# Attention in three wide pieces of 103 keys across heads, with values brought by DMA and masked, whole-tile passes on VectorE, and the output bias as a product

## What is computed

```python
q, k, v = project(norm(x)), project(ctx), project(ctx)    # heads: (32, 16, 128, 8), (32, 16, 77, 8)
scores = q @ k.T / sqrt(8)                                # (32, 16, 128, 77); masked in layer 3
weights = softmax(scores, -1)
o = (weights @ v).merge_heads()                           # (32, 128, 128)
x = x + gate * (o @ Wo + bo)                              # bo in layers 1 and 3
```

## Time and profile before

| | |
|---|---|
| median of three runs | 1613.0 us (1606.56 to 1613.46) |
| profiled execution, own time | 1609.98 us |
| its span | 1608.2 us |
| busy: TensorE, VectorE, GpSimd, ScalarE | 1233.3, 1004.2, 888.1, 821.8 us |
| mean granted TensorE clock | 0.883 of 2.4 GHz |
| l1x, first transfer or table load to last aggregate | 221.2 to 393.7 us |
| l2x | 754.3 to 926.7 us |
| l3x | 1034.2 to 1228.3 us |

### The profile page before, as it was taken

The page is one execution under the profiler, slowest core; times in us unless marked ns, Lnnn a source line. Parts: engine busy times, 40 slices in busy tenths (PEclk is TensorE's granted clock), DMA queues, the critical chain, the costliest instruction groups (busy, mean ns, idle before and its releaser), DMA issues. The chain is left out here.

```text
span 1608.2 us, 27318 instructions
## 1 busy us (share of the span) xinstructions
PE 1233.3 (77%) x9890; PEld 857.0 (53%) x9890; DVE 1004.2 (62%) x2128; ACT 821.8 (51%) x1584; POOL 888.1 (55%) x1106
## 2 busy tenths in 40 slices
PE   4773569997459996444899968689997774989994
PEld 4432546664359994333566535455656553565553
DVE  5789869995531111344999769688882687443421
ACT  2487448886635453144788766467775431212120
POOL 5200148885245554651677578367775345478775
PEclk9796779999679998667899979889997795999997
DMA  2000000000238883110000000000000004344442
GB/s 102 7 0 0 1 2 2 2 2 5 59 111 240 238 230 85 40 31 9 2 1 2 2 16 1 2 2 1 2 2 1 24 33 146 76 80 97 94 88 23
DMA packets 51798, 74.98 MB, mean 47 GB/s; under 512 B 8169, under 2 KB 31602, under 8 KB 51282
## 3 DMA queue, kind: packets, MB, share of 16 engines
q1 hardware_dynamic: 35858, 55.01, 10.7%
q0 software_dynamic: 15808, 18.24, 6.8%
HBM read 57.09 MB, written 16.12 MB: 46 GB/s over the span
## 5 line engine op out<-in xcount | busy, mean ns | idle before, releaser
L1616 PE MATMUL ps<-topk_up_sb,topk_wu 128*128 128x512 f32 x256 | 124.1, 632 | 2.9 <-DVE sb_xnT L1736 2.2
L1517 ACT ACTIVATE topk_ga<-ps 128x512 f32<-128x512 f32 x64 | 38.3, 599 | 155.5 <-PE ps L1616 152.7
L1440 POOL DMA_INDIRECT out<-topk_shared,l3f_route_slots x64 | 100.2, 1566 | 18.1 <-issue 18.0
L1736 DVE TENSOR_TENSOR sb_xnT<-topk_ga,ps 128x512 f32<-128x512 f32 x64 | 43.9, 688 | 103.3 <-ACT topk_ga L1517 99.7
L207 POOL TENSOR_SCALAR sb_stage<-sb_x,l0f_rstd,l0f_shift 128x128 f32<-128x128 f32 x48 | 24.6, 525 | 146.3 <-DVE l0f_shift L194 146.1
L2095 DVE TENSOR_TENSOR l1f_g_y<-ps,l1f_g_wd 128x256 f32<-128x256 f32 x39 | 16.6, 425 | 136.1 <-PE ps L2038 100.2
L2065 ACT ACTIVATE l1f_g_h<-ps,l1f_g_wd 128x256 f32<-128x256 f32 x156 | 63.3, 475 | 73.6 <-DMA l1f_g_wd<-l1f_W 49.9
L522 POOL TENSOR_TENSOR l3x_prob<-l3x_prob,l3x_rden 128x1232 f32<-128x1232 f32 x32 | 72.0, 2249 | 51.1 <-DVE l3x_rden L674 51.1
L522 POOL TENSOR_TENSOR l2x_prob<-l2x_prob,l2x_rden 128x1232 f32<-128x1232 f32 x32 | 72.0, 2249 | 44.4 <-DVE l2x_rden L674 44.4
L634 ACT ACTIVATE l3x_pt<-ps 77x512 f32<-77x512 f32 x128 | 72.7, 592 | 39.7 <-PE ps L576 39.7
L522 POOL TENSOR_TENSOR l1x_prob<-l1x_prob,l1x_rden 128x1232 f32<-128x1232 f32 x32 | 72.0, 2249 | 32.5 <-DVE l1x_rden L674 32.5
(11 more groups left out here) (500 smaller groups left out, 3588.5 us busy)
## 6 DMA issues: line engine op xcount, KB each, us to landing
l1f_g_wd<-l1f_W SPq DMA_DIRECT2D x39, 322.0 KB
l1f_g_wu<-l1f_W SPq DMA_DIRECT2D x39, 256.0 KB
topk_wu<-l3f_W SPq DMA_DIRECT2D x16, 512.0 KB
l1f_y_rows<-l1f_g_y SPq DMA_DIRECT2D x39, 128.0 KB
topk_wd<-l3f_W SPq DMA_DIRECT2D x16, 256.0 KB
...
```

Of the source, the lines that this page charges most:

```text
L1440: pool.indirect_dma_start(out=out_rows, out_offset=spot(g, i), in_=y[g % 2][:, i, :], in_offset=None, compute_op=ALU.add).then_inc(y_added ...
L1517: sc.activation(gx[c % 2][:], ps[:, 2 * (c % 2), :], ACT.Gelu).then_inc(x_acted, 1)
L1616: ins = pe.matmul(ps[:, 2 * (c % 2) + i, :], wu[g % W][:, (i * CX + c) * P:(i * CX + c + 1) * P], xgT[g % 2][:], start=True, stop=True)
L1736: v.tensor_tensor(xh[g % 2][:, c, :], gx[c % 2][:], ps[:, 2 * (c % 2) + 1, :], ALU.mult).then_inc(x_ready, 1)
```

## The change

- **Pieces.** The 308 weights of a group's four heads are cut into pieces of 103, 103 and 102, across the borders of the heads. A piece is turned in four transposes of 103 (or 102) columns, copied as 103 x 512, and weighed in one product a group. There are three pieces in place of four.
- **Values.** For the product of a piece its rows must hold the values of (head, key) in the piece's order. Seven DMAs for each group of four tiles, from SyncE, copy rows of `vall` within SBUF to `vrows` (103 rows, 3 pieces, 4 tiles x 128 columns; two buffers). GpSimd multiplies them by a mask (`vmask`, made once in a stage by six instructions) into `vpad`, 103 x 384, with all features of heads other than the row's own set to zero. The padded values and their clearing in `constants` go.
- **VectorE.** Maximum, subtraction and sum are one instruction of 1232 elements each, and so is the exponential on ScalarE. The statistics' first step moves between maximum and subtraction, the second between sum and reciprocal.
- **Bias.** The bias row is loaded to one partition; a product of a row of ones with it goes ahead of the output product in PSUM. GpSimd's addition of the bias goes, and its wait for the load; TensorE waits for the load once, ahead of the loop.

The core of the diff:

```diff
+    PIECES, L = 3, 103
+    FROM = [(0, 0, 0, 77), (0, 77, 0, 26), (1, 0, 26, 51), (1, 51, 0, 52), (2, 0, 52, 25), (2, 25, 0, 77), (2, 102, 0, 1)]
+    MV = 4
...
-        pt, oT = sbs("pt", [KEYS, HG, GROUPS, P], 2), sbs("oT", [P, P], 2)
+        pt, oT = sbs("pt", [L, PIECES, GROUPS, P], 2), sbs("oT", [P, P], 2)
...
-        bo, gb = sbs("bo", [P, D], 1)[0], sbs("gb", [P, D], 1)[0]
+        vrows, vpad, gated = sbs("vrows", [L, PIECES, MV * P], 2), sbs("vpad", [L, PIECES, P], 2), sbs("gated", [P, D], 2)
+        own_head, vmask = sbs("own_head", [L, PIECES, HG], 1)[0], sbs("vmask", [L, PIECES, P], 1)[0]
+        bo = sbs("bo", [1, D], 1)[0]
...
+        scores = ps[:, 2:6, 0:GK].rearrange("p b (h k) -> p b h k", k=KEYS)
+
+        def piece(g, c):
+            return slice(GK * g + L * c, GK * g + min(L * c + L, GK))
...
+            for j in range(NT // MV):
+                if j >= 2:
+                    sp.wait_ge(vpad_ready, MV * (j - 1))
+                for c, row, key, n in FROM:
+                    sp.dma_start(vrows[j % 2][row:row + n, c, :], t["vall"][key:key + n, j * MV * P:(j + 1) * MV * P]).then_inc(v_here[j % 2], 16)
...
                     pool.wait_ge(heads_made, n - 1)
-                pool.tensor_copy(bass.AP(tensor=vpad[n % 2], offset=0, ap=[[HEADS * 32, KEYS], [HG * 32, GROUPS], [32 + HD, HG], [1, HD]]),
-                                 t["vall"][:, n * P:(n + 1) * P].rearrange("k (g i c) -> k g i c", g=GROUPS, i=HG)).then_inc(vpad_ready, 1)
+                j = n // MV
+                if n % MV == 0:
+                    pool.wait_ge(v_here[j % 2], 16 * len(FROM) * (j // 2 + 1))
+                pool.tensor_tensor(vpad[n % 2][:], vrows[j % 2][:, :, (n % MV) * P:(n % MV + 1) * P], vmask[:], ALU.mult).then_inc(vpad_ready, 1)
...
-            def bias(n):
-                xb = t["x"][:, n * P:(n + 1) * P]
-                pool.tensor_tensor(xb, xb, gb[:], ALU.add).then_inc(biased, 1)
...
-            if bias_out:
-                pool.wait_ge(loads, 16)
-                pool.tensor_scalar(gb[:], bo[:], t["gate"][:, gate_at:gate_at + 1], None, ALU.mult).then_inc(gb_ready, 1)
-                pool.wait_ge(gb_ready, 1)
+            step = Chain(pool, mask_step)
+            step(pool.memset(own_head[:], 1.0))
+            step(pool.affine_select(out=own_head[:], in_=own_head[:], compare_op=ALU.is_ge, fill=0.0, base=0,
+                                    pattern=[[L, PIECES], [-KEYS, HG]], channel_multiplier=1))
+            step(pool.affine_select(out=own_head[:], in_=own_head[:], compare_op=ALU.is_ge, fill=0.0, base=KEYS - 1,
+                                    pattern=[[-L, PIECES], [KEYS, HG]], channel_multiplier=-1))
+            for c in range(PIECES):
+                step(pool.tensor_copy(vmask[:, c, :].rearrange("k (g i c) -> k g i c", g=GROUPS, i=HG),
+                                      own_head[:, c, :].unsqueeze(1).unsqueeze(3).broadcast_to([L, GROUPS, HG, HD])))
...
-            def turn(n, r):
-                if r == 0:
+            def turn(n, c):
+                if c == 0:
                     pe.wait_ge(normed, n + 1)
-                if 4 * n + r >= 2:
-                    pe.wait_ge(turned_kept, 4 * n + r - 1)
+                k = PIECES * n + c
+                if k >= 2:
+                    pe.wait_ge(turned_kept, k - 1)
+                weights = prob[n % 4][:].rearrange("p h k -> p (h k)")
                 for g in range(GROUPS):
-                    ins = pe.transpose(ps[0:KEYS, 6 + r % 2, g * P:g * P + P], prob[n % 4][:, HG * g + r, :], t["ident"][:])
+                    at = piece(g, c)
+                    ins = pe.transpose(ps[0:at.stop - at.start, 6 + k % 2, g * P:g * P + P], weights[:, at], t["ident"][:])
                 ins.then_inc(turned, 1)
 
-            def weigh(n, r):
-                if r == 0:
+            def weigh(n, c):
+                if c == 0:
                     pe.wait_ge(vpad_ready, n + 1)
                     if n >= 1:
                         pe.wait_ge(heads_kept, n)
-                pe.wait_ge(turned_kept, 4 * n + r + 1)
+                pe.wait_ge(turned_kept, PIECES * n + c + 1)
+                rows = min(L, GK - L * c)
                 for g in range(GROUPS):
-                    ins = pe.matmul(ps[32 * g:32 * g + 32, 0, 0:P], vpad[n % 2][:, HG * g + r, :], pt[n % 2][:, r, g, :],
-                                    start=(r == 0), stop=(r == HG - 1), tile_position=(0, 32 * g))
-                if r == HG - 1:
+                    ins = pe.matmul(ps[32 * g:32 * g + 32, 0, 0:P], vpad[n % 2][0:rows, c, 32 * g:32 * g + 32], pt[n % 2][0:rows, c, g, :],
+                                    start=(c == 0), stop=(c == PIECES - 1), tile_position=(0, 32 * g))
+                if c == PIECES - 1:
                     ins.then_inc(heads_made, 1)
...
                 if n >= 1:
                     pe.wait_ge(out_kept, n)
-                pe.matmul(OUT, oT[n % 2][:], w[:, 384:512], start=True, stop=True).then_inc(out_made, 1)
+                if bias_out:
+                    pe.matmul(OUT, t["ones"][0:1, :], bo[:], start=True, stop=False)
+                pe.matmul(OUT, oT[n % 2][:], w[:, 384:512], start=not bias_out, stop=True).then_inc(out_made, 1)
...
@@ -604,19 +616,16 @@
                 weigh(n, 0)
                 turn(n, 2)
                 weigh(n, 1)
-                turn(n, 3)
-                weigh(n, 2)
                 if n + AHEAD < NT:
                     score(n + AHEAD)
-                weigh(n, 3)
+                weigh(n, 2)
...
             def exponent(n):
-                for i in range(2):
-                    sc.wait_ge(shifted, 2 * n + 1 + i)
-                    sc.activation(prob[n % 4][:, 8 * i:8 * i + 8, :], prob[n % 4][:, 8 * i:8 * i + 8, :], ACT.Exp, scale=scale).then_inc(exped, 1)
+                sc.wait_ge(shifted, n + 1)
+                sc.activation(prob[n % 4][:], prob[n % 4][:], ACT.Exp, scale=scale).then_inc(exped, 1)
...
-                for r in range(HG):
-                    if r == 2 and n >= 1:
+                for c in range(PIECES):
+                    if c == 2 and n >= 1:
                         keep_out(n - 1)
-                    sc.wait_ge(turned, 4 * n + r + 1)
-                    sc.activation(pt[n % 2][:, r, :, :].rearrange("k h q -> k (h q)"), ps[0:KEYS, 6 + r % 2, :], ACT.Copy).then_inc(turned_kept, 1)
+                    k, rows = PIECES * n + c, min(L, GK - L * c)
+                    sc.wait_ge(turned, k + 1)
+                    sc.activation(pt[n % 2][0:rows, c, :, :].rearrange("k g q -> k (g q)"), ps[0:rows, 6 + k % 2, :], ACT.Copy).then_inc(turned_kept, 1)
...
+            def largest(n):
+                v.wait_ge(scored, n + 1)
+                v.tensor_reduce(rowmax[n % 2][:].rearrange("p (b h) -> p b h", h=HG), scores, X, ALU.max).then_inc(maxed, 1)
+
             def shift(n):
-                v.wait_ge(scored, n + 1)
-                for i in range(2):
-                    v.tensor_reduce(heads(rowmax[n % 2], i), scores(i), X, ALU.max).then_inc(maxed, 1)
                 if n >= 4:
-                    v.wait_ge(turned, 4 * (n - 3))
-                for i in range(2):
-                    v.wait_ge(maxed, 2 * n + 1 + i)
-                    v.tensor_tensor(probs(n, i), scores(i), heads(rowmax[n % 2], i).unsqueeze(3).broadcast_to([P, 2, HG, KEYS]),
-                                    ALU.subtract).then_inc(shifted, 1)
+                    v.wait_ge(turned, PIECES * (n - 3))
+                v.wait_ge(maxed, n + 1)
+                v.tensor_tensor(prob[n % 4][:].rearrange("p (b h) k -> p b h k", h=HG), scores,
+                                rowmax[n % 2][:].rearrange("p (b h) -> p b h", h=HG).unsqueeze(3).broadcast_to([P, GROUPS, HG, KEYS]),
+                                ALU.subtract).then_inc(shifted, 1)
 
             def total(n):
+                v.wait_ge(exped, n + 1)
+                v.tensor_reduce(rowsum[n % 2][:], prob[n % 4][:], X, ALU.add).then_inc(summed, 1)
+
+            def invert(n):
                 if n >= 2:
                     v.wait_ge(normed, n - 1)
-                for i in range(2):
-                    v.wait_ge(exped, 2 * n + 1 + i)
-                    v.tensor_reduce(rowsum[n % 2][:, 8 * i:8 * i + 8], prob[n % 4][:, 8 * i:8 * i + 8, :], X, ALU.add).then_inc(summed, 1)
-                v.wait_ge(summed, 2 * n + 2)
+                v.wait_ge(summed, n + 1)
                 v.reciprocal(rden[n % 2][:], rowsum[n % 2][:]).then_inc(recip, 1)
 
...
             for n in range(NT):
-                if n + AHEAD - 1 < NT:
-                    shift(n + AHEAD - 1)
-                if n >= 2:
-                    spread(n - 2)
-                if n + AHEAD - 2 < NT:
-                    total(n + AHEAD - 2)
-                if n >= 2:
-                    joined(n - 2)
+                ahead, behind = n + AHEAD - 1, n - 2
+                if ahead < NT:
+                    largest(ahead)
+                if behind >= 0:
```

(9 more changed lines are left out.)

30 lines of the change are left out of this document (10 added, 20 removed).

## The result

| | before | after |
|---|---|---|
| median | 1613.2 us (1606.56 to 1616.44, 4 runs) | 1570.2 us (1563.68 to 1574.30, 4 runs) |
| ratio, 95% interval | | 0.9743 (0.9705 to 0.9781) |
| profiled execution, own time | 1609.98 us | 1574.3 us |
| its span | 1608.2 us | 1572.5 us |
| busy: TensorE, VectorE, GpSimd, ScalarE | 1233.3, 1004.2, 888.1, 821.8 us | 1184.8, 985.9, 935.2, 772.4 us |

The change makes the kernel 43 us faster, where the forecast was 55.5 us against the profiled execution (1555, range 1547 to 1572). The time lies within the range, but 2 us from its upper end and nearer to the 1571 of rival (b) than to 1555; the gain is some 12 us short.

A forecast was written before the change was run, and what follows sets the result against it. VectorE was taken to set the pace in l1x and l2x, with TensorE equally full, and TensorE in l3x. Loops 40.8, starts 2.9 and ends 11.8 sum to 55.5 us off 1609.98, so 1555, range 1547 to 1572.

The forecast's parts named there:

- rival (b): Ring or unseen wait costs more: l3x at 4.85 us gives 1562, 0.2 us in all three stages 1571; chance 0.15.
- Both engines had to become shorter: Attention tile before: VectorE and TensorE each fill 4.84 us, so both must shrink or nothing is won.
- So VectorE sets the pace: l1x before the change: VectorE, without idle time, sets the tile's 4.84 us; l2x taken as the same.
- VectorE at 4.53 us: New attention tile: three whole passes of 1.35 us, statistics, reciprocal and aggregate sum to 4.53 us, against 4.84.
- GpSimd at 4.26 us, the product at 1.0: New tile on GpSimd: with the 103 x 384 product at 1.0 us, 4.26 us, hidden below 4.53.
- Rival (a): GpSimd becomes the bound: product at 1.37 us, tile 4.63, 6.8 us less gain, so 1562; chance 0.13.
- The transfers at nothing: Seven transfers a group, 462 KB, take 1.9 us of 18 us with two buffers; costed at nothing.
- rival (d): TensorE idles in the loops, its clock falls to 1.2 GHz: slower than before, 1653; chance 0.04.
- The bias product: TensorE in l1x and l3x: the single-row addition, 0.2 us, fits in a wait for ScalarE; at worst costs 0.2.
- The ring in l3x at 4.58 us: l3x: maximum and statistics 1.54, subtraction 1.43, signal 0.10, mask and score 1.51 sum to a 4.58 us tile.
- The ends: Stage end, last subtraction to last aggregate, TensorE alone: 17.9 us becomes 13.9, about 11.8 us gained in three stages.
- The starts: Stage start: VectorE's 1.24 us wait for tile 4's scores shortens by 0.95; 2.9 us in three stages.

## Why the prediction was right, and where it was short

- **Both engines had to become shorter**: right for the full gain. One alone gains nothing (VectorE's), or 0.11 us a tile (TensorE's). "So VectorE sets the pace" was wrong: TensorE set it, with 4.83 us against VectorE's own 4.72. The forecast did not suffer, since the new pace was reckoned from the new passes.
- **VectorE at 4.53 us**: right, 4.54, and TensorE now waits for the subtraction: the scores start 0.14 us behind its end, after 0.21 us without work in l1x and 0.57 in l2x. (The profile puts most of this down to the keys of GpSimd, which had been ready a tile earlier.) The price of a whole pass (1.35 us) was met by 1.29 to 1.35. What I had too small was the engine's wait for its own result, 0.10 us by the half sums of before: behind a whole pass it is 0.2, twice a tile. It didn't disturb the sum, because the new order covers it.
- **GpSimd at 4.26 us, the product at 1.0**: right; 1.01 long, and 4.23 a tile. Rival (a) did not come. The estimate of 0.83 us by the Trainium skill's "GPSIMD Engine Reference", section 3.1, was lower than what was measured.
- **The transfers at nothing**: right in the loops, and still so at twice the number, though they are a third larger and three times as long as reckoned.
- **The clock**, rival (d): did not come. It stayed at 1.00, 2.4 GHz, in all three loops, with TensorE busy 98.45 of 118 us in l2x. The rule of the Trainium skill's "TensorE: Matmul & The Clock Gate", Part 4, that transposes do not count had no effect to be seen in the loops, with a quarter of turns and products gone. At the ends it did fall: in the last 3.4 us of l1x, with TensorE busy for 1.45 of them, the granted clock was 0.60 on average, and over the end of l2x 0.97. In l3x it was 1.00 to the end, and the ends of l1x and l3x differ by less than 0.1 us.
- **The bias product: this is the step that failed.** "The addition, 0.2 us by the 0.39 that the output's two passes occupy, fits in this wait" holds for a product with 128 rows, as the run with 128 rows shows to the hundredth. The product that the change makes has one row. That keeps its weights and those of the output from being loaded ahead, and the way from turns to weighing is 1.88 us instead of 1.52: 0.36 where I had nothing, or 0.2 at worst. Of these 0.36 the tile of l3x shows 0.27 (4.90 against 4.63), since below that the ring holds it. In l1x the loop hides it, as VectorE sets the pace. In l3x TensorE has nothing to spare: the loop gave back 15.6 us where I had 24.0, and 22.7 with 128 rows. At the ends of l1x and l3x, where TensorE works off the last tiles alone, it is 15.8 us instead of 13.9.
- **The ring in l3x at 4.58 us**, just above the two engines' own work: 4.63 or 4.64 with the bias out of the way, and then it is this ring, term by term (1.56, 1.43, 0.14 and 1.51 us for my 1.54, 1.43, 0.10 and 1.51). In the changed kernel it isn't reached: the mask products start 0.40 us behind the subtraction's end. Rival (b) named the place and the size of the loss, 4.85 us, but with paths that hold one another up as its mechanism. The mechanism was one instruction. That the range, drawn wide for another reason, held the time is luck in part.
- **The ends**, 13.9 us: 13.7 in l2x, which has no bias, and 13.9 in l1x without it. **The starts** gave 2.0 us in three stages, not 2.9; runs of the changed kernel differ by as much there (58.2 to 59.1).

The account: 55.5 forecast; the loops were short by 9.8 (40.8 to 31.0), the ends by 3.4 (11.8 to 8.4), the starts by 0.9 (2.9 to 2.0), and the last maximum and subtraction took 0.4 more, which leaves 41.0. With 128 rows in the bias product the stages give 52.2 (against the kernel before on the first chip), and the forecast is missed by 3.
